# Layer 2's last node stage, moved into its second edge pass

## The chip, the cores and the metric

The kernel runs on one NeuronCore of a Trainium2 chip, in one launch. The metric is the device time of that launch in microseconds (us). The engines of the core run their own instruction streams and wait for one another through semaphores: TensorE (PE, matmuls into the eight PSUM banks; PEld is its weight loads), VectorE (DVE), ScalarE (ACT), GpSimd (POOL) and SyncE (SP, which here only issues DMAs). TensorE's clock is granted by the chip at one of two levels, 1.2 and 2.4 GHz; the profile shows it as 0.50 and 1.00.

## The reference

Four graph layers on one graph of 3125 nodes with 128 features and 50000 edges, sorted by destination. Each layer normalizes its input, applies ReLU, runs a graph operator and adds the result to x. Layer 0 sums weighted neighbours, layer 1 means of neighbours, layer 3 is a diffusion of nine steps over the adjacency, and layer 2 is the one that changes here: two sublayers, each with an eight-headed attention part and a relational part. The second sublayer, cut to what matters:

```python
for h in range(8):                                   # attention part, mean over the heads
    Wh = x1 @ W[h]
    e = leaky_relu((Wh @ a_src[h])[src] + (Wh @ a_dst[h])[dst], 0.2)
    outs.append(segment_sum(seg_softmax(e, dst)[:, None] * Wh[src], dst))
x1 = mean(outs)
deg = segment_sum(w, dst)                            # relational part
x2 = relu(segment_sum((w / maximum(deg[dst], 1e-16))[:, None] * (x2 @ Wc)[src], dst))
x = x + maximum(x1, x2)
h = maximum(layernorm(x), 0)                         # what layer 3 (the diffusion) starts from
```

## The kernel before

Nodes lie in 25 blocks of 128 (the last has 53), edges in 392 chunks of 128. SBUF is one large array, `arena`, addressed by words; `banks` is PSUM.

**An edge pass** is `layer2_edges(i, begin)` (L1439), run once with i = 0 and once with i = 1. GpSimd gathers a chunk's source rows by an indirect DMA (L229, called from L1502) into a ring of 40 chunks, and waits for the sums of chunk c-40 (L1501). SyncE loads the destination terms and indices of a batch of eight chunks (L1515, L1519), three and two batches deep. Batches pass through a chain: one-hot windows and flags (VectorE, L1533 to L1552), logits (L1568), their transpose (PE L1697, ACT L1782), maxima by two scans (L1578, L1584), the exchange at the batch edges (PE L1707 to L1712), `exp` (ACT L1786), transpose back (PE L1719), `spread` of the attention values over the window of 17 nodes (DVE L1618). Then TensorE sums a chunk: in the second pass L1736 (eight heads, 136 columns), L1737 (relational part, 17 columns) and L1739 (softmax sums and degrees, 17 columns); in the first pass L1733 and L1734 (17 columns each) and L1739. ScalarE copies the finished windows into the accumulators `ACC` (nine planes, one for each head and one for the relational part, features by nodes) and `SACC` (L1820, L1823), seven chunks later. All engines walk the same hand-written order of slots, ten to a batch, so that sums of a batch stand some three batches behind its gathers, and each engine works strictly in order.

In the second pass TensorE also runs matmuls whose results nobody reads: `busy` (L1671 to L1675) multiplies an identity into bank 7, with 24 x 512 columns at the start, 3 x 512 a slot until the first sums, and after each chunk's sums 512 + 256 columns:

```python
                            sums(c)
                            busy(512, 256)
```

**The node stage** `layer2_end(begin, ends)` (L2292) starts when all sums of the pass are stored. TensorE first turns `SACC` for all 25 blocks (L1864, 50 instructions), VectorE makes reciprocals (L1869, L1871, L2419). Then block by block: nine products of 128 x 128 x 128 (eight heads with `Wg`, one with `Wc`: L2349, L2352, L2353, L2355, two instructions each), six scalings and a ReLU on ScalarE (L2371, L2374, L2376), two more heads and the sum tree on VectorE (L2426, L2430, L2433, L2435), the maximum (L2438), the residual on GpSimd (L2406), and the layer norm over groups of four blocks (DVE L2444 to L2456, ACT L2381, L2387). `spans` are these groups. SyncE stores the new x by groups (L2326) and brings the adjacency counts back from DRAM over the dead accumulators in five pieces (L2321, L2323, L2330, L2332, L2336, and L2574 in the next stage); `PIECES`, `SOURCES` and `RETURNED` (L2277 to L2280) say which source blocks come with which piece and in which order the diffusion's first step uses them.

**The diffusion** (`diffusion`, L2485) multiplies the adjacency counts (25 source blocks, four ranges of destinations) by the scaled features in nine steps: PE L2640, L2644, L2646. Its first step takes rows that GpSimd, ScalarE and VectorE prepare from the norm's result (L2601, L2699, L2771). `weights_t` (L2218) spreads the softmax of t over TB (PE L2233, DVE L2250) ahead of the second pass; of TB only its last row is read on this path (L2601).

`any_stages` (L3242) is another path, for graphs whose edges are spread too widely; it does not run here.

## Time and profile before

| | |
|---|---|
| median of 3 runs | 2660.73 us (2654.13 to 2671.45) |
| the profiled execution | 2652.48 us, span 2650.7 us, mean granted clock 0.783 |
| busy: PE, PEld | 2346.3 us (89%), 1958.4 us (74%) |
| busy: DVE, ACT, POOL | 1452.3 us (55%), 1208.4 us (46%), 1198.2 us (45%) |
| gathers (L229), second pass | x392, 392.2 us busy |
| PEclk in 40 slices of 66.3 us, tenths of 2.4 GHz | 9856566588755555555698697888899999999999 |

The second edge pass lies at about 1324 to 1873 us of the span, the node stage behind it until 1961, the diffusion until the end. Busy is the time in which an engine had an instruction under way; TensorE's matmuls are pipelined and their ends modelled, so a TensorE that is busy all the time need not stream columns all the time. In a row of a timeline or chain, the first number is the start, the second the duration, x the number of merged instructions, and what stands in brackets the idle time before and who ended it. A group's row gives the busy sum and the mean in ns.

### The profile page before, as it was taken

The numbers are of one execution on the slowest core, as the hardware profiler recorded it, in microseconds if no ns is written. First come the engines' busy times: TensorE is split into PE (matmuls) and PEld (weight loads), VectorE is DVE, ScalarE is ACT, GpSimd is POOL, SyncE is SP. The second block draws the span as 40 slices with busy tenths as digits, with TensorE's granted clock in tenths as the row PEclk, the third lists the DMA queues.
The fourth block names the chain that finished last, engine by engine and source line by source line (L and its number), as shares of the span: only waits on it lengthen the run. The fifth ranks groups of instructions, "written<-read, shape, count | busy, mean of one in ns | idle before, by whom it ended". The sixth has DMA issues, their size and how long they took to land.

```text
span 2650.7 us, 51792 instructions
## 1 busy us (share of the span) xinstructions
PE 2346.3 (89%) x12833; PEld 1958.4 (74%) x12833; DVE 1452.3 (55%) x6161; ACT 1208.4 (46%) x5256; POOL 1198.2 (45%) x1268
## 2 busy tenths in 40 slices
PE   3778778787549999999899999999979999999998
PEld 2555556554339999999857777777878899888887
DVE  5656556578536666666436566665564333344443
ACT  3666667675313333333314343343674444444443
POOL 3777777700067777775077777775131000000000
PEclk9856566588755555555698697888899999999999
DMA  3242442431244444443244344443272000000002
GB/s 90 61 125 64 123 125 64 125 103 42 66 111 113 110 109 108 109 110 106 53 110 110 100 111 108 109 108 85 68 283 83 14 22 18 25 25 25 25 25 61
DMA packets 172291, 227.45 MB, mean 86 GB/s; under 512 B 63503, under 2 KB 131160, under 8 KB 171736
## 3 DMA queue, kind: packets, MB, share of 16 engines
q0 software_dynamic: 50176, 131.74, 18.8%
q1 hardware_dynamic: 114350, 88.60, 11.1%
q10 hardware_dynamic: 7466, 3.73, 0.5%
q8 instruction: 114, 1.87, 0.3%
q14 instruction: 185, 1.52, 0.2%
HBM read 183.63 MB, written 40.29 MB: 84 GB/s over the span
## 4 chain that ended last, share of the span: by engine, by line
PE 71%; issue 7%; DVE 7%; POOL 5%; ACT 4%; DMA 4%; ACTq 2%; DVEq 0%; SPq 0%; POOLq 0%
PE banks L2644 10%; PE banks L2640 10%; PE banks L1675 7%; PE banks L1733 7%; PE banks L1734 6%; POOL arena L229 5%; PE banks L1736 4%; PE banks L1739 3%; PE banks L2646 3%; PE banks L733 2%; PE banks L945 2%; PE banks L1737 2%; DMA arena<-h_table,arena 2%; PE banks L736 2%; PE banks L1691 1%
## 5 line engine op out<-in xcount | busy, mean ns | idle before, releaser
L229 POOL DMA_INDIRECT arena<-value_table,arena x392 | 387.2, 988 | 318.2 <-DMA ed_table<-arena 199.1
L2640 PE MATMUL banks<-counts,u_parts 128*128 128x448 f32 x1323 | 491.7, 372 | 9.6 <-DVE u_parts L2771 9.6
L2644 PE MATMUL banks<-counts_even,u_parts 128*128 128x448 f32 x1323 | 486.3, 368 | 0.0
L229 POOL DMA_INDIRECT arena<-gat_table,arena x392 | 392.2, 1001 | 207.3 <-issue 88.0
L229 POOL DMA_INDIRECT arena<-h_table,arena x392 | 376.3, 960 | 119.4 <-issue 88.4
L2819 DVE CAST counts_even<-counts 128x448 fp32r<-128x448 bf16 x450 | 163.9, 393 | 304.1 <-PE banks L2644 276.1
L733 PE MATMUL banks<-arena 128*128 128x425 bf16 x392 | 198.3, 506 | 84.6 <-ACT arena L789 77.5
L2640 PEld LDWEIGHTS banks<-counts,u_parts 128*128 128x128 f32 x1323 | 249.6, 189 | 30.3 <-issue 9.7
L736 PEld LDWEIGHTS banks<-arena 128*128 128x128 f32 x784 | 211.1, 293 | 80.9 <-issue 72.7
L2644 PEld LDWEIGHTS banks<-counts_even,u_parts 128*128 128x128 f32 x1323 | 249.5, 189 | 20.7 <-ACT counts_even L2747 0.2
L1675 PE MATMUL banks<-arena 128*128 128x256 bf16 (+1 forms) x967 | 262.8, 370 | 1.7 <-DVE arena L2250 1.7
L1734 PE MATMUL banks<-arena 128*128 128x17 f32 x784 | 230.8, 376 | 0.0
L1733 PE MATMUL banks<-arena 128*128 128x17 f32 x784 | 227.2, 371 | 0.0
L786 ACT ACTIVATE arena<-banks 128x400 f32 x392 | 207.9, 530 | 37.2 <-DVE banks L722 26.5
L1820 ACT ACTIVATE arena<-banks 128x32 f32 (+1 forms) x784 | 186.0, 237 | 62.5 <-issue 39.2
L1734 PEld LDWEIGHTS banks<-arena 128*128 128x128 f32 x784 | 214.3, 334 | 0.0
L2747 ACT ACTIVATE counts_even<-counts 128x896 fp32r<-128x896 bf16 x123 | 117.4, 954 | 209.3 <-PE banks L2644 196.6
L1808 ACT ACTIVATE arena<-banks 128x2 f32<-128x2 f32 (+1 forms) x262 | 45.6, 174 | 357.5 <-PE banks L1739 304.3
L1733 PEld LDWEIGHTS banks<-arena 128*128 128x128 f32 x784 | 202.2, 319 | 6.2
L736 PE MATMUL banks<-arena 128*128 128x17 f32 x784 | 174.9, 304 | 35.1 <-DMA arena<-h_table,arena 34.2
L1736 PE MATMUL banks<-arena 128*128 128x136 f32 x784 | 187.5, 325 | 0.0
L722 DVE TENSOR_TENSOR banks<-banks,arena 128x26 f32<-128x26 f32 x391 | 75.7, 194 | 184.4 <-ACT arena L778 180.0
(301 smaller groups left out, 4758.5 us busy)
## 6 DMA issues: line engine op xcount, KB each, us to landing
adj_rows<-arena SPq DMA_DIRECT2D x5, 4000.0 KB
counts<-adj_rows SPq DMA_DIRECT2D x2, 7200.0 KB, 21.6
arena<-ed_table SPq DMA_DIRECT2D x784, 0.5 KB
arena<-turned_rows SPq DMA_DIRECT2D x27, 448.0 KB, 3.4
arena<-h_table,arena POOLq DMA_INDIRECT x392
arena<-value_table,arena POOLq DMA_INDIRECT x392
arena<-gat_table,arena POOLq DMA_INDIRECT x392
counts<-adj_rows SPq DMA_DIRECT2D x2, 1600.0 KB, 6.2
```

Of the source, the lines that this page charges most:

```text
L229: return e.indirect_dma_start(into, None, table, bass.IndirectOffsetOnAxis(ap=index.bitcast(U32), axis=0))
L733: e.matmul(banks[:, c % RBANK, W1:CS], BY_LO[:, kx, :], BY_HI_D[:, kx, 0:CC], start=True, stop=True, skip_group_check=True)
L736: e.matmul(banks[:, c % RBANK, 0:W1], G[:, k, :], S[:, c // BC % 2, c % BC, :], start=False, stop=True, skip_group_check=True).then_inc(l0 ...
L786: e.activation(first.of(C, j), windows_in(j)[:, 1:, 0:WIN], ACT.Copy, scale=SMALL).then_inc(l0_counted, 1)
L1675: e.matmul(banks[:, 7, 0:n], identb, spare[:, 0:n], start=True, stop=True, skip_group_check=True)
L1733: e.matmul(pv[:, 0, :], rows[:, 0:D], OHF[k3][:, j, :], start=begins, stop=True, skip_group_check=True)
L1734: e.matmul(pv[:, 1, :], rows[:, D + H:], OHV[k3][:, j, :], start=False, stop=True, skip_group_check=True)
L1736: e.matmul(pv[:, 0:H, :], rows[:, 0:D], S[c % RS][:, 0:H, :], start=begins, stop=True, skip_group_check=True)
L1820: e.activation(first.of(acc, c), sums_in(c)[:, :, 0:WIN], ACT.Copy).then_inc(e2_acc, 1)
L2640: e.matmul(banks[:, 2 * r, 0:HALFW], weight, C_odd[:, w0:w0 + HALFW], start=start, stop=stop)
L2644: x = e.matmul(banks[:, 2 * r + 1, 0:HALFW], weight, tile(n), start=start, stop=stop)
L2819: e.tensor_copy(into, counts).then_inc(d_even_dve, 1)
```

## The change

- `EndNodes` takes the place of `Ends` and holds the node stage as small steps per block: `products` (three groups of matmuls: heads 0 to 2 with the block's own turn of `SACC`, heads 3 to 6, head 7 and the relational part), `weigh`, `scaled` (three groups of ScalarE scalings that write over the block's own columns of `ACC`), `summed` (the sum tree over `ACC`, maximum, residual, statistics, all on VectorE), and per span `variances`, `root`, `scales`, `normed`.
- `layer2_edges(1, ...)` calls these steps for blocks 0 to 22 within its slots. `first[b]` is the chunk at which block b's steps begin: the chunk after which all its sums are stored, plus eight. Blocks 23 and 24 stay behind the pass, in `layer2_end`. All early blocks use bank 7, one group at a time; the two late ones have banks of their own.
- `busy(512, 256)` after a chunk's sums is called only for chunks below `first[0]`, which is 30. From there on no unread products run.
- x is loaded and stored by spans on SyncE's queue within the pass. The end weights are loaded at the start of the pass, and divided by H there (before: the reciprocals were). GpSimd has no part in the stage any more.
- The counts come back in other pieces: blocks 0 to 12 even when five spans are normed; 18 to 23 when the sums are done; 1 to 17 odd after the last residual; 24 after the last store; 14 and 16 in the diffusion. The order of the sources follows.
- `weights_t` makes only the last row of TB on this path.

```diff
             def sp(e):
                 begin(e)
                 first = Windows(e, FI, f"e2w_{i}")
+                if i:
+                    nodes.begin_sp(e)
                 for b in range(NBATCH):
+                    if i:
+                        for g in nodes.sp_at(b):
+                            nodes.x_store(e, g)
+                            nodes.x_load(e, g + 1)
...
             def dve(e):
...
+                if i:
+                    nodes.begin_dve(e)
                 for p in range(NBATCH + 4):
+                    if i and p == 1:
+                        nodes.degrees(e)
                     for q in range(SLOTS):
                         c = chunk_at.get(SLOTS * p + q)
                         if c is not None:
                             spread(c)
                             if c % PER == 1 and c > 3 * PER:
                                 share(c // PER - 2)
+                            if i:
+                                for b, c0 in nodes.first.items():
+                                    if c == c0 + 2:
+                                        nodes.weigh(e, b)
+                                    if c == c0 + 8:
+                                        nodes.summed(e, b)
+                                        if b % 4 == 3 and b < 20:
+                                            nodes.variances(e, b // 4)
+                                    if c == c0 + 12 and b % 4 == 3 and b < 20:
+                                        nodes.scales(e, b // 4)
...
             def pe(e):
...
                             sums(c)
-                            busy(512, 256)
+                            if not i or c not in nodes.waiting:
+                                if not i or c < nodes.first[0]:
+                                    busy(512, 256)
+                            else:
+                                for b, k in nodes.pe_at(c):
+                                    nodes.products(e, b, k)
...
             def act(e):
...
+                            if i:
+                                for b, k in nodes.act_at(c):
+                                    nodes.scaled(e, b, k)
+                                for b, c0 in nodes.first.items():
+                                    if b % 4 == 3 and b < 20 and c == c0 + 10:
+                                        nodes.root(e, b // 4)
+                                    if b % 4 == 3 and b < 20 and c == c0 + 13:
+                                        nodes.normed(e, b // 4)
...
-        PIECES = [(23, 24), tuple(range(0, 18, 2)), tuple(range(1, 18, 2)) + (22,), (18, 19), (20, 21)]
-
-        SOURCES = PIECES[1] + PIECES[2] + PIECES[0] + PIECES[3] + PIECES[4]
+        PIECES = [tuple(range(0, 14, 2)), tuple(range(18, 24)), tuple(range(1, 18, 2)), (24,), (14, 16)]
+        SOURCES = PIECES[0] + PIECES[1][:3] + PIECES[2] + PIECES[1][3:] + PIECES[3] + PIECES[4]
...
+        class EndNodes:
...
+                self.first = {b: block_end(b) + 8 for b in range(self.EARLY)}
+                self.waiting = {c + k for c in self.first.values() for k in range(7)}
 
...
+            def products(self, e, b, part):
+                weight_sums, eight, last = self.places(b)
+                if part == 0:
+                    if b == 0:
+                        e.wait_ge(d_scales, 2)
+                    elif b < self.EARLY:
+                        self.bank_free(e, b - 1)
+                    e.wait_ge(e2_sacc, NC + block_end(b))
+                    e.matmul(weight_sums, SACC[0:3 * (H + 1), b * P:(b + 1) * P], add_parts[0:3 * (H + 1), :], start=True, stop=True, skip_group_check=True)
+                elif b < self.EARLY:
+                    e.wait_ge(self.copied.sem, self.copied.at(3 * b + part))
+                if part < 2:
+                    for h in ((0, 1, 2), (3, 4, 5, 6))[part]:
+                        x = e.matmul(eight[h], self.own(h, b), end_Wg[:, h, :], start=True, stop=True, skip_group_check=True)
+                else:
+                    e.matmul(last[0], self.own(H - 1, b), end_Wg[:, H - 1, :], start=True, stop=True, skip_group_check=True)
+                    x = e.matmul(last[1], self.own(H, b), end_Wc, start=True, stop=True, skip_group_check=True)
+                x.then_inc(self.product.sem, 1)
+
+            def bank_free(self, e, b):
+                e.wait_ge(self.copied.sem, self.copied.at(3 * b + 3))
+
+            def scaled(self, e, b, part):
+                weight_sums, eight, last = self.places(b)
+                SV = self.SV[b % 2]
+                e.wait_ge(self.product.sem, self.product.at(3 * b + part + 1))
+                if part == 0:
+                    e.wait_ge(self.weighed.sem, self.weighed.at(b + 1))
+                if part < 2:
+                    for h in ((0, 1, 2), (3, 4, 5, 6))[part]:
+                        x = e.activation(self.own(h, b), eight[h], ACT.Copy, scale=SV[:, h:h + 1])
+                else:
+                    e.activation(self.own(H - 1, b), last[0], ACT.Copy, scale=SV[:, H - 1:H])
+                    x = e.activation(self.own(H, b), last[1], ACT.Relu, scale=SV[:, H:H + 1])
+                x.then_inc(self.copied.sem, 1)
+
+            def weigh(self, e, b):
+                do, settle = dve_own.do, lambda: dve_own.settle(e)
+                SV = self.SV[b % 2]
+                e.wait_ge(self.product.sem, self.product.at(3 * b + 1))
+                do(e.tensor_scalar_max(SV, self.places(b)[0], 1e-16))
+                settle()
+                e.reciprocal(SV, SV).then_inc(self.weighed.sem, 1)
+
+            def summed(self, e, b):
+                do, settle = dve_own.do, lambda: dve_own.settle(e)
+                g = self.span_of(b)
+                x = self.XB[:, b - self.SPANS[g][0], :]
+                heads = lambda h, n: ACC[:, h:h + n, b * P:(b + 1) * P]
+                e.wait_ge(self.copied.sem, self.copied.at(3 * b + 3))
+                for n in (4, 2, 1):
+                    do(e.tensor_tensor(heads(0, n), heads(0, n), heads(n, n), ALU.add))
+                    settle()
+                do(e.tensor_tensor(self.own(0, b), self.own(0, b), self.own(H, b), ALU.max))
+                e.wait_ge(self.x_in.sem, self.x_in.at(16 * (g + 1)))
+                settle()
+                e.tensor_tensor(x, x, self.own(0, b), ALU.add).then_inc(self.added.sem, 1)
+                e.wait_ge(self.added.sem, self.added.at(b + 1))
+                do(e.bn_stats(self.stats[b % 2], x))
+                settle()
+                do(e.bn_aggr(self.mv[:, b, :], self.stats[b % 2]))
+
...
+            def begin_dve(self, e):
+                e.tensor_scalar_add(dinv2l, indeg, 1.0).then_inc(self.var.sem, 1)
+                e.wait_ge(self.weights.sem, self.weights.at(32))
+                e.tensor_scalar_mul(end_Wg, end_Wg, 1.0 / H).then_inc(d_scales, 1)
+
...
+            def sp_at(self, batch):
+
+                return [g for g in range(self.NS - 1) if (self.first[4 * g + 3] + 13) // BC + 6 == batch]
+
+            def pe_at(self, c):
+                return [(b, k) for b, c0 in self.first.items() for k in range(3) if c == c0 + 3 * k - k // 2]
+
+            def act_at(self, c):
+                return [(b, k) for b, c0 in self.first.items() for k in range(3) if c == c0 + 2 * k + 2]
+
+        def layer2_end(ends):
...
+            LATE = (NB - 2, NB - 1)
+            G_LATE = ends.NS - 1
...
+                e.wait_ge(ends.made.sem, ends.made.at(G_LATE))
+                returned(0, 0, 7, 0)
+                e.wait_ge(e2_mm, 2 * NC)
+                e.dma_start(counts[:, words(18, 24)], adj_rows[:, words(18, 24)]).then_inc(ends.back[1].sem, 16)
+                e.wait_ge(ends.added.sem, ends.added.at(NB))
+                returned(2, 0, 9, 1)
+                ends.x_store(e, G_LATE)
...
```

## Rows read from the trace of the kernel before

**Rows 1.** Stages: window, length, each engine's busy us (instructions), clock, DMA share, GB/s.

```profile
120.00:540.00 420.00, 323.57 (x1454) 235.61 (x1452) 253.56 (x1322) 278.34 (x1137) 315.37 (x330) 0.60 0.35 102
780.00:1240.00 460.00, 460.00 (x2327) 431.94 (x2327) 283.80 (x1466) 168.50 (x1240) 351.59 (x356) 0.50 0.43 113
1360.00:1438.00 78.00, 78.00 (x580) 58.88 (x578) 46.88 (x232) 29.02 (x187) 59.90 (x60) 1.00 0.42 109
1446.00:1498.00 52.00, 52.00 (x241) 39.77 (x242) 22.93 (x115) 14.25 (x93) 36.71 (x38) 0.50 0.39 101
...
1360.00:1873.00 513.00, 500.82 (x3417) 387.69 (x3414) 305.85 (x1536) 200.87 (x1314) 365.05 (x364) 0.87 0.39 101
...
1873.00:1961.00 88.00, 67.24 (x501) 64.44 (x501) 64.16 (x230) 64.04 (x223) 16.21 (x29) 0.88 0.53 182
1961.00:2650.00 689.00, 670.95 (x3387) 609.46 (x3387) 268.62 (x753) 300.69 (x588) 23.62 (x47) 0.99 0.13 41
```

**Rows 2.** Chain of waits, 1360 to 1873, its shares by line.

```profile
by line: PE banks L1675 35.7%; PE banks L1736 22.1%; PE banks L1737 10.3%; PE banks L1739 8.0%; DMA arena<-gat_table,arena 3.4%; issue 3.4%; POOL arena L229 2.8%; PE banks L1697 2.1%; PE banks L1707 1.9%; PE banks L1691 1.7%; PE banks L1719
```

**Rows 3.** The gathers of the second pass, their source line.

```profile
L229 POOL DMA_INDIRECT arena<-gat_table,arena x392: 940/946/2021, 1324.4 to 1839.6; - x196
  issue: 88.0, 289
  PE banks L1739: 35.8, 102
```

**Rows 4.** Line L1739 in the window 1100 to 2100.

```profile
L1739 PE MATMUL banks<-arena x534: 181/183/197, 1100.8 to 1872.3; 128*27 128x17 bf16 x178
```

**Rows 5.** Chain of waits, 1873 to 1962.

```profile
1875.63 10.83 PE banks L1864 x50
...
1890.98 1.14 ACT arena L2371 x4
...
1958.51 1.25 ACT arena L2387 x3
...
1960.77 0.70 PE banks L2640
```

**Rows 6.** Timeline of TensorE in the node stage.

```profile
1886.39 2.07 PE L2349 MATMUL banks<-arena 128*128 128x128 f32 x8
1888.26 1.06 PE L2352 MATMUL banks<-arena 128*128 128x128 f32 x4
...
1889.88 1.06 PE L2349 MATMUL banks<-arena 128*128 128x128 f32 x8
```

**Rows 7.** Groups by line, 1873 to 1961.

```profile
L2426 DVE TENSOR_TENSOR arena<-arena 128x384 f32<-128x384 f32 x25 | 13.8, 551 | 2.0 <-ACT arena L2374 2.0
...
L2438 DVE TENSOR_TENSOR arena<-arena 128x128 f32<-128x128 f32 x25 | 7.3, 292 | 2.6
...
L2362 ACT ACT_TABLE_LOAD x1 | 1.3, 1283 | 0.0
```

**Rows 8.** DMA issues, 1870 to 2100: KB each, us to landing.

```profile
counts<-adj_rows SPq DMA_DIRECT2D x2, 7200.0 KB, 21.6
```

**Rows 9.** Timeline of TensorE ahead of the clock's fall.

```profile
1440.75 0.30 PE L1697 MATMUL banks<-arena 128*64 128x128 f32 x1 [1.18 <-DVE arena L1570]
```

**Rows 10.** Windows of line L1739 alone, one instruction per chunk.

```profile
780.00:1240.00 460.00, 68.58 (x351) 35.15 (x351) 0.50 0.43 113
1360.00:1406.00 46.00, 5.65 (x31) 2.83 (x31) 1.00 0.41 109
```

**Rows 11.** Timeline of TensorE in the first pass.

```profile
1000.79 0.61 PE L1733 MATMUL banks<-arena 128*128 128x17 f32 x2
1001.24 0.59 PE L1734 MATMUL banks<-arena 128*128 128x17 f32 x2
```

**Rows 12.** Timeline of TensorE in the second pass, low clock.

```profile
1463.01 0.82 PE L1736 MATMUL banks<-arena 128*128 128x136 f32 x2
1463.63 0.45 PE L1737 MATMUL banks<-arena 128*128 128x17 f32 x2
```

More of the change, by code:

```diff
@@ L2216, in build, with weights_t @@
         U_parts = rounded("u_parts", U_at, UW)
-        def weights_t(begin, bank, room):
+        def weights_t(begin, bank, room, rows=tuple(range(STEPS))):
             def sp(e):
@@ new lines, in home, with own, places @@
+            def home(self, b):
+                if b < 12:
+                    return self.own(H - 1, b)
+                return self.spare if b == 12 else self.own(H, b - 13)
+            def own(self, h, b):
+                return ACC[:, h, b * P:(b + 1) * P]
+            def places(self, b):
+                n = {NB - 2: (7, 0, 2), NB - 1: (3, 4, 5)}.get(b, (7, 7, 7))
+                first = [banks[:, n[0], (q + 1) * D:(q + 2) * D] for q in range(3)]
+                second = [banks[:, n[1], q * D:(q + 1) * D] for q in range(4)]
+                return banks[:, n[0], 0:H + 1], first + second, [banks[:, n[2], q * D:(q + 1) * D] for q in range(2)]
```

294 lines of the change are left out of this document (121 added, 173 removed).

## The prediction

> **What bounds the kernel now.** I read the stages first, then the chain of waits inside the stage that changes, then single instructions. The stage table [rows 1] shows two edge passes of the same loop and the node stage behind the second one. The first pass (780 to 1240 shown) has TensorE busy for all 460 us at a granted clock of 0.50, that is 1.2 GHz. The second (1360 to 1873) takes 513 us, with TensorE busy 501, VectorE 306 and ScalarE 201. Then comes the node stage from 1873 to 1961, then 689 us of diffusion. The chain through the second pass [rows 2] is TensorE nearly everywhere, and its largest item is L1675, the products that nobody reads (35.7%). Behind TensorE stands a second limit that is nearly as near: the gathers [rows 3]. One takes 0.946 us and is followed by 0.30 us (88.0 us in 289 cases), so 1.25 us a chunk. The 392 gathers start between 1324.4 and 1839.6, against 391 x 1.25 = 489 us at their own pace: they lose only 26 us to TensorE.
>
> So taking work from TensorE in the pass can win little there. The change has two separate effects: the 88 us behind the pass shrink, and TensorE inside the pass gets other work and perhaps another clock.
>
> **Removed behind the pass.** The last L1739 of the pass starts at 1872.3 [rows 4], the first diffusion product at 1960.77 [rows 5]: 88.5 us. What stays: the last stores to the accumulators until 1875.6, where L1864 begins [rows 5] (3.3 us); two blocks of products; one block's scaling, sums and norm. A block's products are 9 matmuls, each two instructions. At the low clock eight of them run from 1886.39 to 1888.26 [rows 6], 1.87 us, so 18 take 4.2, plus two of the 50 of L1864 (10.83/50 each), 0.43: 4.7 us. From 1889.88 the same eight take 1.06 in place of 2.07: such a run brought the clock back within 3.5 us, so the second block costs about half: 7.2 for both. ScalarE's last two scalings are 0.6 (four take 1.14, [rows 5]). The sums of a block on VectorE: a 384-wide add is 0.551, a 128-wide one 0.292 [rows 7], hence 0.68 + 0.42 + 3 x 0.29 for the tree, the maximum and the residual, and 0.45 for statistics and aggregation (my estimate, from the 128-wide row): 2.4, with the waits between them 2.6. Then the root with its table load (1.28, [rows 7]; Exp is used in the pass, so it is loaded anew) 1.5, inverse and shift 0.7, five norms 2.1 (three take 1.25, [rows 5]) and 1.1 to the first diffusion product. Sum 3.3 + 7.2 + 0.6 + 2.6 + 1.5 + 0.7 + 2.1 + 1.1 = 19 us. **Gain: 69 us**, whatever happens in the pass.
>
> The diffusion's input moves too. Its returned pieces are now seven blocks issued before the pass ends, six when the sums are done, nine after the last residual. A piece of nine takes 21.6 us [rows 8]; diffusion consumes a source block in 689/(9 x 25) = 3.06 us and reaches the nine as its eleventh source, 31 us after its start, while they are issued 5 us before it. That is covered by 14 us: 0; without that cover the rest of the 21.6 would show.
>
> **Added inside the pass, with no clock change.** Per block (16 chunks) TensorE gets 18 + 2 instructions, ScalarE nine scalings (2.6 us), a share of root and norm and of two table loads (some 1.2), VectorE 2.6 plus 0.5 for the weights. ScalarE at 201 of 513 us and VectorE at 306 of 513 carry that. The SP queue gets two weight loads, six x loads and five stores; the stores wait for a norm that is due one or two batches before the queue's loads are needed (three buffers), so nothing: if that cover went, it would be a landing of some 2 us per group of blocks, 10 us in all. begin on VectorE waits for the end weights (issued first), hidden by the first batch of gathers. The t-weights shrink from ten products to one; nobody on the path waits: 0. The POOL queue loses the 25 residual adds, off the path here.
>
> **The clock in the pass is the disputed term.** Removed from chunk 30 on: 512 + 256 columns a chunk. What do the traces show of TensorE without them? The first pass is the same loop without such products, and 0.50 all the way, with TensorE 100% busy [rows 1]. The first stage (120 to 540) has a 425-column product per chunk and 0.60. The second pass with them has 1.00 from 1360 to 1438, and 0.50 from 1446 to 1498 [rows 1], busy in both: after one gap of 1.18 us before L1697 [rows 9] the clock went down, and it was still down at 1498, 52 us on, though each chunk carried its sums and its 768 extra columns. So even with the extra products the clock is barely held. Without them a chunk's sums stream less than half as much, and the new products come in runs of three, four and two heads, 0.9 to 1.9 us at the low clock, with whole chunks between. The run that brought the clock back behind the pass [rows 6] was up to 3.5 us of nothing else. I take 0.50 for nearly all of the pass from chunk 30 on.
>
> The Trainium skill's page "TensorE: Matmul & The Clock Gate", in the table of "Why this matters for your kernels", asks only that there be no long idle gap, longer than any that this pass would have, between bursts of matmuls. By it the clock would stay up here, which is the first rival. The trace does not agree: the clock fell behind a gap of 1.18 us [rows 9], and was low through a pass without one.
>
> **TensorE's pace at 0.50.** The first pass did 351 chunks in 460 us [rows 10]: 1.311 a chunk, 20.97 for 16. The second pass has the same weight loads and wider moving sides. Where no unread product stands before it, L1736 takes 0.62 until L1737 starts, against 0.45 from L1733 to L1734; L1737's two last 0.45, L1734's 0.59 [rows 11, 12]: +0.17 - 0.14 = +0.03 a chunk, so 21.5. With a block's products (4.7): 26.2 us for 16 chunks, where the gathers need 20.0. TensorE is then the bound by a wide margin.
> One more wait: VectorE runs a block's sums in one piece at chunk c0+8, after ScalarE's last scaling, and queued behind it are flags, one-hot and scans, and the next spreads, for which TensorE waits. TensorE has about three chunks of work ready then (3.4 us); VectorE needs the scaling (1.2), 2.6, and a handful of its own operations. I put 1.5 us a block, between 0 (hidden, as VectorE was until now) and 2.6 (the whole piece exposed), nearer the upper end because those operations come on top.
>
> 27.7 x (362/16 = 22.6) = 627 us from chunk 30, which is at 1405.8 (the 31st L1739 starts just before 1406, [rows 10]); less 3 us for the first stretch at the high clock: the sums end at 2030 instead of 1873. **Loss: 157 us.**
>
> **Sum.** 157 - 69 = +88 us on the profiled execution's 2652.5 (span 2650.7 and 1.8 around it): 2740. That execution is 8 us under the median of the three runs shown (2660.7) and inside their spread; I leave it at **2740 us**, 3% slower. With the stall at 0: -34; at 2.6: +25. So this case spans 2705 to 2770.
>
> **Rival 1, the clock holds (faster).** If the products of the finished blocks and the sums together keep 1.00, TensorE needs under 15 us for 16 chunks (0.91 a chunk now at that clock, less the unread ones, plus 2.5) and the gathers set the pace: the last one starts between 1814 and 1840 and the sums end 25 us later (33 now, less 0.25 for each of the last 30 chunks). Diffusion begins 17 to 19 us on, between 1857 and 1883, 78 to 104 us earlier: 2549 to 2575, say 2562. For it: the 0.60 of the first stage, where node products also lie between the chunks, and the 0.88 of the node stage. Against it: the first pass and the fall at 1442 [rows 1, 9]. The skill's page named above speaks for it. It decides from where about half of the 16-chunk stretches run at the gathers' 20.0: (1960.8 - 19 - 1405.8)/22.6 = 23.7 us a stretch is break-even between 27.7 and 20.0. Chance 0.18.
>
> **Rival 2, a mixed clock.** The runs of products lift it now and then, as in the first stage. With a third of the stretches at 20.0: 25.1 on average, 567 us, sums end at 1973, diffusion at 1992: 31 later: 2684 (2650 to 2705). For it: the 0.60 of the first stage. Against it: that stage streams 425 columns a chunk at one pass and 512-wide products, the new one has no such width. Chance 0.12.
>
> **Rival 3, the waits are worse than priced.** weigh, scaled and the three product groups each wait on another engine through one bank (7), so that a wait of 1 us at each of the three would add 23 x 3 = 69 us to the low-clock case: over 2775. Nothing in the trace speaks for it; enough chunks lie between the steps. Chance 0.04.
>
> The forecast has the rest, 0.66.
>
> **How the numbers follow.** A measurement of this kernel can tell about 1%, 27 us. Faster by more than that (under 2634): rival 1, 0.18. Within (2634 to 2687): about half of rival 2 and a little of the forecast's lower edge, 0.08. Slower: 0.74. The range must leave out rival 1 whole; it reaches from rival 2's lower end to a little beyond the forecast's upper bound, 2650 to 2780. The forecast's own range is 2705 to 2770.
>
> **What would show it.** Granted clock in the pass: 0.50 for nearly all of it (rival 1: near 1.0). Gathers: the last one starts near 2000, and their idle time before a launch is given to L1739, several hundred us in place of 35.8. From the last L1739 to the first L2640: 19 us. TensorE's waits on VectorE before the spreads: 1.5 us a block. The prediction fails if the clock holds for more than half of the pass, or if the pace at the low clock without the unread products is not that of the first pass.

## The result, and the profile after

| | us, median | ratio to before, 95% |
|---|---|---|
| before | 2657.43 (2649.32 to 2671.45) | 1 |
| after | 2739.27 (2737.97 to 2742.29) | 1.0304 (1.0258 to 1.0350) |
| forecast | 2740 (2650 to 2780) | |

The change makes the kernel 3% slower. The ratios, here and below, leave out executions in the slower state that the chip sometimes shows (one of run 10's ten, at 2685.11 us), and need not be the quotients of the medians. The profiled execution of after has a span of 2737.1 us, 86.4 more than the 2650.7 of before. Line numbers have moved: L1736, L1737 and L1739 of before (a chunk's sums) are L1762, L1763 and L1765 now.

The stages of after, in the columns of [rows 1]:

```profile
780.00:1240.00 460.00, 459.61 (x2319) 431.05 (x2319) 281.90 (x1463) 168.13 (x1235) 351.83 (x356) 0.50 0.43 113
1360.00:1406.00 46.00, 45.05 (x312) 32.67 (x316) 23.60 (x117) 13.07 (x84) 35.04 (x37) 0.99 0.43 112
1406.00:1600.00 194.00, 181.12 (x897) 169.92 (x895) 111.25 (x525) 80.83 (x458) 115.31 (x118) 0.52 0.34 89
1600.00:1800.00 200.00, 182.63 (x915) 171.82 (x915) 113.83 (x538) 86.75 (x475) 114.12 (x117) 0.53 0.34 88
1800.00:2000.00 200.00, 183.46 (x916) 172.68 (x915) 112.41 (x526) 87.21 (x476) 95.07 (x96) 0.53 0.36 103
2047.00:2737.00 690.00, 671.34 (x3387) 609.23 (x3387) 268.48 (x754) 301.15 (x588) 24.08 (x47) 0.99 0.13 42
```

Up to chunk 30 the clock is as in [rows 1]; the chunk itself comes at 1408.4, 2.6 us later than the 1405.8 of before. From there the granted clock is 0.52 to 0.53 where the whole pass before had 0.87. It is 0.50 from 1412.5 on, but for four short rises of 6.8 us each; two of them, and a stretch between:

```profile
1610.50:1617.00 6.50, 3.78 (x31) 3.39 (x29) 4.47 (x18) 2.87 (x17) 4.60 (x5) 1.00 0.30 78
1617.50:1692.00 74.50, 70.53 (x347) 66.48 (x346) 42.35 (x203) 32.84 (x179) 42.53 (x43) 0.50 0.35 90
1692.50:1699.00 6.50, 3.93 (x32) 3.54 (x31) 4.54 (x19) 2.85 (x17) 4.64 (x5) 1.00 0.32 83
```

The diffusion is as it was: 690 us at 0.99. The pass ends later, and what follows it is short. The last of the sums:

```profile
L1765 PE MATMUL banks<-arena x784: 182/195/196, 770.4 to 2028.0; 128*27 128x17 bf16 x196
```

The timeline of TensorE behind it, up to the first diffusion product (L2732):

```profile
2030.77 0.56 PE L2392 MATMUL banks<-arena 27*128 27x9 f32 x2 [2.62 <-ACT arena L1856]
2031.27 3.35 PE L2397 MATMUL banks<-arena 128*128 128x128 f32 x14
...
2035.93 2.39 PE L2397 MATMUL banks<-arena 128*128 128x128 f32 x14
...
2047.15 0.71 PE L2732 MATMUL banks<-counts,u_parts 128*128 128x448 f32 x1 [8.39 <-DVE u_parts L2862]
```

The sums end 155.7 us later than in [rows 4] (1872.3), and 19.2 us lie behind them in place of 88.5: +155.7 - 69.3 = +86.4, the whole difference of the spans.

The gathers, which answer to [rows 3], with what ended GpSimd's idle time before them in this pass, and TensorE's waits between 1406 and 2028 (engine, line, what it waited for: us in all, times, longest):

```profile
L229 POOL DMA_INDIRECT arena<-gat_table,arena x392: 940/946/1806, 1325.2 to 1963.2; - x196
  PE banks L1765: 194.4, 212
```

```profile
PE banks L1762 <- DVE arena L1630: 30.5, 23, 2.8
PE banks L1765 <- DVE arena L1643: 14.4, 43, 1.1
PE banks L1745 <- ACT arena L1819: 2.9, 3, 1.5
```

A gather is as fast as before (946 ns at the median), but the last one starts 124 us later: they now follow TensorE, for which they wait 194.4 us in place of 35.8. TensorE waits once per finished block for spread weights from VectorE (L1630), and a little for the split weights (L1643). Most of the waits for L1630 are of 1.05 to 1.27 us; four, each at the end of one of the short rises of the clock, are of 2.40 to 2.77.

### The profile page after: what moved, and what is told of

The parts are those of the page before. It is cut to its first block, busy times and chain, and to the rows that moved or that the text cites. A ratio compares the mean times of both kernels' runs of the same rounds, so it can differ in the third digit from the quotient of the medians.

```text
span 2737.1 us, 50328 instructions
## 1 busy us (share of the span) xinstructions
PE 2392.2 (87%) x12048; PEld 2082.9 (76%) x12091; DVE 1462.8 (53%) x6184; ACT 1236.2 (45%) x5318; POOL 1176.5 (43%) x1243
## 4 chain that ended last, share of the span: by engine, by line
PE 70%; DVE 9%; issue 8%; ACT 4%; POOL 4%; DMA 3%; ACTq 1%; DVEq 0%; SPq 0%; POOLq 0%
PE banks L2736 9%; PE banks L2732 9%; PE banks L1759 6%; PE banks L1760 6%; PE banks L1762 6%; POOL arena L229 4%; PE banks L1765 3%; PE banks L2397 3%; PE banks L2738 3%; PE banks L733 2%; PE banks L945 2%; PE banks L1763 2%; DMA arena<-h_table,arena 2%; PE banks L1717 2%; PE banks L736 2%
## 5 line engine op out<-in xcount | busy, mean ns | idle before, releaser
L229 POOL DMA_INDIRECT arena<-gat_table,arena x392 | 386.1, 985 | 336.5 <-PE banks L1765 194.4
L2732 PE MATMUL banks<-counts,u_parts 128*128 128x448 f32 x1323 | 491.2, 371 | 8.4 <-DVE u_parts L2862 8.4
L1762 PE MATMUL banks<-arena 128*128 128x136 f32 x784 | 283.7, 463 | 30.5 <-DVE arena L1630 30.5
L2732 PEld LDWEIGHTS banks<-counts,u_parts 128*128 128x128 f32 x1323 | 249.2, 188 | 29.5 <-issue 8.6
L736 PEld LDWEIGHTS banks<-arena 128*128 128x128 f32 x784 | 211.7, 293 | 71.3 <-issue 61.7
L1762 PEld LDWEIGHTS banks<-arena 128*128 128x128 f32 x784 | 194.3, 304 | 39.8 <-DVE arena L1630 32.6
L1760 PEld LDWEIGHTS banks<-arena 128*128 128x128 f32 x784 | 214.2, 333 | 0.0
L1759 PEld LDWEIGHTS banks<-arena 128*128 128x128 f32 x784 | 202.1, 319 | 6.5
L1763 PEld LDWEIGHTS banks<-arena 128*128 128x128 f32 x784 | 207.0, 316 | 0.0
## 6 DMA issues: line engine op xcount, KB each, us to landing
counts<-adj_rows SPq DMA_DIRECT2D x1, 7200.0 KB, 21.4
```

The costliest lines, as they stand in the source:

```text
L229: return e.indirect_dma_start(into, None, table, bass.IndirectOffsetOnAxis(ap=index.bitcast(U32), axis=0))
L736: e.matmul(banks[:, c % RBANK, 0:W1], G[:, k, :], S[:, c // BC % 2, c % BC, :], start=False, stop=True, skip_group_check=True).then_inc(l0 ...
L1759: e.matmul(pv[:, 0, :], rows[:, 0:D], OHF[k3][:, j, :], start=begins, stop=True, skip_group_check=True)
L1760: e.matmul(pv[:, 1, :], rows[:, D + H:], OHV[k3][:, j, :], start=False, stop=True, skip_group_check=True)
L1762: e.matmul(pv[:, 0:H, :], rows[:, 0:D], S[c % RS][:, 0:H, :], start=begins, stop=True, skip_group_check=True)
L1763: e.matmul(pv[:, H, :], rows[:, D + H:], S[c % RS][:, H, :], start=False, stop=True, skip_group_check=True)
```

## The experiments

All ratios are to the kernel before, run on the same chip. "The pass" is the second edge pass; runs 7 and 8, on a chip apart, stand in their section.

| kernel | us | ratio, 95% | clock in the pass | last sums product |
|---|---|---|---|---|
| 1: unread products kept in 9 of 16 chunks | 2784.28 | 1.0467 (1.0425 to 1.0510) | 0.50 to 0.57 | 2086.4 |
| 2: before, without unread products | 2667.77 | 1.0038 (1.0015 to 1.0060) | 0.50 to 0.52 | 1886.5 |
| 3: VectorE's sum two chunks later | 2732.17 | 1.0277 (1.0239 to 1.0315) | 0.50 to 0.54 | 2029.1 |
| 4: three of nine products | 2687.68 | 1.0124 (1.0087 to 1.0161) | 0.50 to 0.52 | 1973.0 |
| 5: unread in every chunk | 2805.89 | 1.0532 (1.0477 to 1.0586) | 0.62 to 0.71 | 2105.6 |
| 6: unread in every chunk, wider | 2809.31 | 1.0553 (1.0516 to 1.0589) | 0.69 to 0.71 | 2113.0 |
| 9: the change again | 2738.57 | 1.0298 (1.0253 to 1.0344) | 0.53 | 2027.2 |
| 11: sum in four pieces, no unread | 2707.97 | 1.0174 (1.0130 to 1.0218) | 0.50 to 0.54 | 1998.6 |
| 10: unread and four pieces | 2664.60 | 0.9996 (0.9960 to 1.0032) | 0.85 to 1.00 | 1946.3 |
| 12: unread and pieces off the split | 2603.43 | 0.9785 (0.9761 to 0.9809) | 0.98 to 1.00 | 1887.4 |

### 1. Unread products back in the chunks without node work

```
-    if not i or c < nodes.first[0]:
-        busy(512, 256)
+    if i:
+        for b, c0 in nodes.first.items():
+            if c == c0 + 7:
+                nodes.bank_free(e, b)
+    busy(512, 256)
```

> The changed kernel, with 512 + 256 unread columns again after every chunk's sums outside the seven chunks of a block's products (so in 9 of 16 chunks), TensorE waiting for the block's last scaling before the first of them. Theory (the low clock makes the loss): the granted clock in the pass comes back to 0.8 to 0.9, the sums end near 1880 instead of 2028, the tail of 19 us stays, so about 2590 us (2565 to 2625), faster than the kernel before. Rival A (the stage's clock is low whatever is added, unread products only take time): 201 chunks times 0.45 to 0.64 us more, 2830 to 2870. Rival B (waits between the engines set the pace, the clock does not matter): about 2739, no change.

Measured: 2784.28 us, 45 more than after. The windows (columns as above):

```profile
1406.00:1600.00 194.00, 185.88 (x940) 156.78 (x939) 101.63 (x480) 73.88 (x420) 106.94 (x108) 0.57 0.31 82
1600.00:1800.00 200.00, 196.59 (x933) 164.67 (x933) 104.11 (x488) 79.47 (x431) 104.13 (x104) 0.52 0.30 79
```

The clock stayed low, so my theory of this run was wrong: to undo the removal in nine chunks of sixteen does not undo its effect. The unread products were paid for, at the low clock, but not in full: the pass is 58.4 us longer than that of after (2086.4 against 2028.0), where rival A had 90 to 129, and the time lies between rivals A and B. In the same pass TensorE's waits for L1630 fell from 30.5 to 10.1 us, which is a part of the difference.

### 2. The kernel before, without unread products from chunk 30

```
-    busy(512, 256)
+    if not i or c < 30:
+        busy(512, 256)
```

> The kernel before, with its unread products left out from chunk 30 on and nothing else changed. Theory: the clock falls to 0.50 right behind chunk 30 and TensorE sets the pace with 21.5 us for 16 chunks: 362/16 x 21.5 = 486 us, sums end at 1892 instead of 1873, so +19: about 2675 us (2660 to 2685), a small loss. Rival A (unread products only cost time): the gathers set the pace, sums end between 1840 and 1850, 2625 to 2635. What lies between this and the changed kernel is then the price of the node work at the low clock.

Measured: 2667.77 us, 0.4% slower than before.

```profile
1406.00:1600.00 194.00, 194.00 (x985) 181.66 (x984) 121.24 (x601) 78.26 (x510) 148.31 (x151) 0.52 0.42 110
1600.00:1800.00 200.00, 200.00 (x994) 188.16 (x993) 121.97 (x607) 78.81 (x511) 148.02 (x153) 0.50 0.41 108
1415.00:1886.00 471.00, 471.00 (x2325) 442.72 (x2325) 279.91 (x1389) 184.62 (x1201) 316.69 (x324) 0.50 0.37 98
```

```profile
L1739 PE MATMUL banks<-arena x784: 182/195/196, 772.3 to 1886.5; 128*27 128x17 bf16 x196
```

This is the removal alone, and two things are to be seen. The clock is 0.50 from 1415 to the end of the sums, with TensorE busy in all 471 us: it fell without a wait and did not come back. And the price is only 14.2 us of pass, 4.0 of them ahead of chunk 30 (1409.8 here, 1405.8 in before). The reason is in the pace: at 0.50 the sums alone take 21.4 us for 16 chunks, in each of the twenty stretches of 16 from chunk 46 to 366, about as long as the gathers of before (515.2 us for 391, [rows 3], or 21.1 for 16). So the removal costs little by itself, but it leaves no room for the node products.

### 3. VectorE's sum of a block two chunks later

```
-    if c == c0 + 8:
+    if c == min(c0 + 10, NC - 1):
         nodes.summed(e, b)
```

Root, scales and norms move by two chunks too.

> The changed kernel, with VectorE's sums of a block two chunks later (c0+10, at most chunk 391), the root, inverse and norm two later too. Theory: VectorE no longer waits for ScalarE's last scaling (65 us in the pass in 23 waits), so most of TensorE's 30.5 us of waits for the spreads in the pass goes: 20 to 30 us less, 2710 to 2720. Rival (the spreads are late because of the length of the sums themselves, not of their wait): 0 to 8 us less.

Measured: 2732.17 us, 7 less than after; the rival was right. The wait moved:

```profile
PE banks L1765 <- DVE arena L1643: 36.9, 43, 2.9
```

The waits for L1630 are gone and those for the split weights are 22.5 us longer. The sum is one piece of VectorE's work; wherever it stands whole, something that TensorE needs is queued behind it.

### 4. Three of nine products per block

```
-    for h in ((0, 1, 2), (3, 4, 5, 6))[part]:
+    for h in (((2,), (6,))[part] if b < self.EARLY else ((0, 1, 2), (3, 4, 5, 6))[part]):
```

and the product of head 7 only for the last two blocks. The output is not the layer's.

> The changed kernel, with only three of the nine products of each of the blocks 0 to 22 made (one in each of the three groups; six matmuls a block are left out, and the numbers are not the layer's). Theory (TensorE at the low clock sets the pace): 23 x 12 instructions x 0.234 us = 65 us less, about 2675. Rival B (waits between the engines set the pace): under 15 us less. Rival C (the products lift the clock here and there): the clock of 0.53 in the pass falls to 0.50 and the gain is under 50.

Measured: 2687.68 us, 51.6 less than after, at a clock of 0.50 to 0.52. The pass ends 55.0 us earlier (1973.0), where the theory had 65 for the products left out: TensorE's time for them is on the path, for the most part. Rival C's sign came too: the four short rises of the clock in after are missing here. They were worth little (see the stall, below), and the gain in the pass is above the 50 that this rival had as its bound.

### 5 and 6. Unread products in every chunk

Bank 7 isn't free while node products stand in it, so these multiply by zeros and add to the current bank of sums:

```
+    if i and c >= nodes.first[0]:
+        for n in (384, 384):
+            e.matmul(banks[:, bank_of(c), 0:n], spare[:, 0:P], spare[:, 0:n], start=False, stop=True)
     e.wait_ge(e2_split, nb0 + b + 1)
```

The second kernel has (512, 512) in the seven chunks of a block's node work.

> The changed kernel, with two products of 384 columns (768 columns, as many as in the kernel before) inside the sums of every chunk from the first finished block on, the seven chunks with a block's node work among them. They multiply by zeros and add to the bank of sums that TensorE owns at that moment, ahead of the wait for the split weights, so nothing is changed in the output and no other engine's bank is touched. The run with such products in only 9 of 16 chunks stayed at a granted clock of 0.50 to 0.57 and cost 45 us more than the change. Theory (it is the stretches of seven chunks with fp32 products and nothing wide streamed that lose the clock, so filling them too keeps it): clock 0.80 or more in 1406 to 1800, the gathers are paced by themselves again, the last sums product near 1875 to 1890 (kernel before 1872.3), the work behind the pass 19 us as after the change, so 2590 to 2610 us, faster than the kernel before by about 50 to 65. Rival A (the fp32 products of the node work hold the clock down whatever stands beside them): clock 0.50 to 0.55, every chunk 0.64 us dearer, the pass some 80 us longer than in the changed kernel: 2810 to 2860. Rival B (the clock is up in some stretches and down in others): 0.6 to 0.8, 2640 to 2740.

> As the run with two products of 384 columns in every chunk, but two of 512 columns (1,024) in the seven chunks of a block's node work. If the width beside the fp32 products matters, the clock is higher than in that run (by 0.05 or more in 1406 to 1800), and if the clock is already near 0.99 there, the time is the same within 5 us. If both stay at 0.50 (rival A), it is 15 to 35 us slower than that run, by 7 chunks of 16 times 256 more columns at 1.2 GHz (0.21 us) times 22.6 blocks = 34 us.

Measured: 2805.89 and 2809.31 us. The clock is not low any more, it goes up and down (rival B of the first, at another time than it gave):

```profile
1600.00:1800.00 200.00, 187.89 (x1057) 132.76 (x1055) 106.92 (x506) 79.32 (x436) 105.96 (x108) 0.71 0.31 82
```

The cause of the falls is in the timeline of TensorE, here around 1666:

```profile
1663.43 0.29 PE L1763 MATMUL banks<-arena 128*128 128x17 f32 x2
1663.57 0.49 PE L1766 MATMUL banks<-arena 128*128 128x384 bf16 x2
1663.99 0.18 PE L1768 MATMUL banks<-arena 128*27 128x17 bf16 x1
...
1664.99 0.18 PE L1768 MATMUL banks<-arena 128*27 128x17 bf16 x1
1666.58 0.72 PE L1762 MATMUL banks<-arena 128*128 128x136 f32 x2 [1.40 <-DVE arena L1630]
...
1674.78 0.20 PE L1768 MATMUL banks<-arena 128*27 128x17 bf16 x1
...
1676.54 0.20 PE L1768 MATMUL banks<-arena 128*27 128x17 bf16 x1
```

Before the wait a chunk with its two unread products (L1766) takes 1.00 us, behind it 1.76: windows of 1655 to 1665 and of 1668 to 1680 have a clock of 1.00 and 0.50. VectorE's own timeline says why TensorE waited:

```profile
1662.81 1.48 DVE L2437 TENSOR_TENSOR arena<-arena 128x512 f32<-128x512 f32 x3 [2.04 <-ACT arena L2419]
...
1665.37 0.18 DVE L2446 BATCH_NORM_AGGREGATE arena<-arena 128x2 f32<-128x6 f32 x1
1665.48 0.28 DVE L1560 TENSOR_TENSOR arena<-arena 64x129 f32<-64x129 f32 x1
...
1666.22 0.30 DVE L1630 TENSOR_TENSOR arena<-arena 128x153 f32<-128x153 bf16 x1
```

It waited 2.04 us for ScalarE's last scaled product, then ran the sum in one piece until 1665.55, then four operations of a batch's scan, and only then the spread weights. Between 1406 and 2100 the clock fell 17 times from 1.00 to 0.50, each time at such a wait of 1.40 to 1.62 us (the expectation of run 7 has 18, a miscount). It rose again 20 to 55 us later. Three shorter waits for L1630 at the high clock, of 0.75 to 0.98 us, did not lose it. So two things of the change bear on the clock: with unread products in every chunk it comes back, to stay until the next such wait, with them in 9 of 16 or none it doesn't, but for rises of mostly 7 us; and in run 5 each of these long waits loses it. The wider kernel does nothing more: its mean clock from 1406 to 1800 is 0.70 against 0.68, and its time is 3.4 us longer, no difference.

### 7 and 8. VectorE's sum in four pieces, with and without unread products

The tree's first add, its other two, maximum and residual, and the statistics stand behind the 9th, 10th, 11th and 12th chunk of the block; root, scales and norms follow later.

```
-    if c == c0 + 8:
-        nodes.summed(e, b)
+    for k in range(4):
+        if c == min(c0 + 9 + k, NC - 1):
+            nodes.summed(e, b, k)
```

> As the run with two products of 384 columns in every chunk, and VectorE's sum of a block (2.0 us of waiting for ScalarE's last scaled product and 2.7 us of instructions in one piece behind one chunk) in four pieces, behind the 9th to the 12th chunk of the block, with what hangs on it later. In the run without this, each of the 18 falls of the clock from 1.00 to 0.50 between 1406 and 2086 stands at a wait of TensorE for VectorE's spread weights (L1630) of 1.40 to 1.62 us, one per block, and at 0.50 a chunk with its unread products takes 1.77 us, at 1.00 only 1.0, against 1.28 of a gather's pace. Theory (the stall behind VectorE's sum is what loses the clock, the unread products are what keeps it): the waits are under 1 us, the clock 0.85 or more in 1406 to 2000, the gathers set the pace, last sums product 1875 to 1895, 2590 to 2615 us. Rival A (with that wait gone another of the same length comes in its place, for VectorE's split weights as in the run with the sums two chunks later): clock 0.6 to 0.75, 2760 to 2810. Rival B (the clock falls without such a wait, from the fp32 products): clock under 0.6, 2820 or more.

> The changed kernel (no unread products) with VectorE's sum of a block in the same four pieces. At a clock of 0.50 the waits for VectorE in the pass are 30.5 + 14.4 us of TensorE's time; where the pieces take most of that away, 15 to 30 us less than the changed kernel: 2710 to 2725. The theory says that the clock stays at 0.50 to 0.55 here, as nothing wide is streamed. Rival (without the stalls the clock holds even without unread products): 0.8 or more, 2590 to 2640.

Measured: 2998.01 us (ratio 0.9955, 0.9931 to 0.9978) and 2969.52 (0.9863, 0.9824 to 0.9903), on a chip on which the kernel before takes 3015.11. There all passes are longer, the first one too (its gathers run from 39.7 to 637.3 us, in after from 40.8 to 533.6), though a single gather lasts as long (946 ns at the median). Times of that chip can't be set beside the others, so both kernels were run again, with the change itself.

### 9 to 11. The change, and both kernels again

> The changed kernel itself once more, to stand beside the two other kernels of this call. The last call ran on a chip on which the kernel before takes 3015 us instead of 2655 to 2661, with a third edge pass that is longer than here, so its ratios can't be set against those of the others. Expected where the kernel before takes about 2660: a ratio of 1.026 to 1.035, 2730 to 2750 us. If the chip is the slow one again: near the 0.986 of the kernel with VectorE's sum in four pieces, above it by 0 to 0.01.

> Two products of 384 columns in every chunk and VectorE's sum of a block in four pieces, as in the last call; there the clock was 0.79 in 1600 to 1990 instead of 0.57 without the unread products, and 0.62 to 0.72 with them but with the sum in one piece. Where the kernel before takes 2660: theory (VectorE's stall loses the clock): clock 0.75 to 0.95 in 1500 to 2000, last sums product 1880 to 1960, 2600 to 2680 us. Rival (another wait of over 1 us per block takes its place): clock 0.6 to 0.72, 2760 to 2810 as with the sum in one piece (2805.9).

> The changed kernel with VectorE's sum of a block in four pieces and no unread products, as in the last call, where the clock stayed 0.50 in nearly all of the pass. Where the kernel before takes 2660: 2710 to 2725 us (the 30.5 + 14.4 us of waits for VectorE in the pass mostly gone), clock 0.50 to 0.55. Rival: the waits move as in the run with the sums two chunks later, 2730 to 2740.

Measured: 2738.57, 2664.60 and 2707.97 us. First the pieces without unread products:

```profile
1600.00:1800.00 200.00, 197.68 (x965) 186.91 (x964) 121.82 (x575) 90.72 (x502) 123.54 (x124) 0.50 0.35 92
```

```profile
PE banks L1766 <- DVE arena L1643: 8.5, 23, 1.1
```

30.6 us less than the change, as its theory had it, a little better than the range it gave: the waits for VectorE fell from 30.5 + 14.4 to 8.5 us. The clock is 0.50 although TensorE is busy for 198 of 200 us and its only wait of 0.6 us or more from 1400 to 1980 is one of 1.13 at 1413.44, where the clock fell. Now the same with unread products:

```profile
1406.00:1500.00 94.00, 89.55 (x688) 64.64 (x687) 66.74 (x318) 49.30 (x282) 71.76 (x73) 1.00 0.43 112
1600.00:1800.00 200.00, 192.35 (x1274) 137.37 (x1273) 127.57 (x604) 94.38 (x527) 129.86 (x131) 0.85 0.37 98
```

The clock is up for most of the pass, and the ratio is 0.9996 against 1.0532 with the same unread products and the sum in one piece. That VectorE's sum in one piece cost the clock is shown by this pair (run 5 and run 10): they differ in nothing but where the sum and what hangs on it stand. Eight falls of the clock are left between 1500 and 1910. Four follow a wait for the split weights of 0.94 to 1.20 us, one (1509.92) a wait of 0.98 with no releaser in the profile. The other three follow waits for the split weights of only 0.52 to 0.58, while thirteen more waits for them of 0.51 to 0.62 in the pass had no fall behind them. One of each kind:

```profile
1602.03 0.18 PE L1769 MATMUL banks<-arena 128*27 128x17 bf16 x1 [0.94 <-DVE arena L1643]
...
1628.98 0.18 PE L1769 MATMUL banks<-arena 128*27 128x17 bf16 x1 [0.52 <-DVE arena L1643]
```

The windows around the second:

```profile
1626.00:1631.00 5.00, 4.49 (x37) 3.05 (x38) 4.63 (x20) 1.65 (x12) 4.02 (x4) 1.00 0.42 106
1632.00:1651.00 19.00, 19.00 (x86) 13.97 (x85) 7.25 (x37) 5.08 (x30) 7.96 (x9) 0.50 0.28 73
```

### 12. Pieces kept away from the split weights

```
-    if c == min(c0 + 9 + k, NC - 1):
+    if c == nodes.piece_at(b, k):
...
+    def piece_at(self, b, k):
+        light = [c for c in range(self.first[b] + 10, NC) if c % BC in (2, 3, 4, 5, 6)] + [NC - 1] * 4
+        return light[k]
```

> Two products of 384 columns in every chunk, and the four pieces of a block's VectorE sum placed only behind the third to seventh chunk of a batch of eight, from the block's 10th chunk on, so that none stands in front of the split weights that TensorE needs for a batch's first chunk. In the run with the pieces behind the 9th to 12th chunk five of the falls of the clock between 1500 and 1910 stand at a wait of TensorE for the split weights of 0.94 to 1.20 us, or (1509.92) at one of 0.98 that the profile puts down to no releaser; the last sums product was at 1946.3 there, at 1872.3 in the kernel before. Theory (those waits lose the clock): they fall under 0.6 us, the clock is 0.90 or more in 1500 to 1900, last sums product 1890 to 1925, 2600 to 2640 us, faster than the kernel before. Rival (with the wait gone the products of the node work lower the clock by themselves, or another wait does): clock 0.80 to 0.88, last sums product 1935 to 1960, 2645 to 2670, no different from the kernel before.

Measured: 2603.43 us (2597.75 to 2606.83), ratio 0.9785 (0.9761 to 0.9809). This version is faster than both kernels: by 2.1% (1.9 to 2.4) than before and, by the two ratios (0.9785 / 1.0298), by 5% than the change. The next three views are its windows, its last sums product, and its first diffusion product in the timeline of TensorE.

```profile
1406.00:1500.00 94.00, 91.38 (x694) 66.77 (x695) 68.13 (x328) 49.23 (x280) 72.36 (x72) 0.98 0.42 109
1500.00:1600.00 100.00, 96.25 (x739) 69.59 (x739) 71.74 (x344) 55.16 (x309) 75.81 (x77) 1.00 0.45 118
1600.00:1800.00 200.00, 192.30 (x1482) 139.45 (x1481) 146.22 (x701) 108.16 (x610) 150.51 (x150) 1.00 0.43 112
```

```profile
L1769 PE MATMUL banks<-arena x784: 182/189/197, 768.5 to 1887.4; 128*27 128x17 bf16 x196
```

```profile
1905.51 0.71 PE L2744 MATMUL banks<-counts,u_parts 128*128 128x448 f32 x1 [8.90 <-DVE u_parts L2874]
```

The pass is 15.1 us longer than before (1887.4 against 1872.3, [rows 4]) and what follows takes 18.1 us in place of 88.5, 70.4 less; together -55.3, and the spans differ by 2595.9 - 2650.7 = -54.8. With the clock held, TensorE does the node products beside the gathers, and the gain behind the pass is kept.

What held it is less clear than the time. The theory had the waits for the split weights under 0.6 us, and they aren't: five of 0.70 to 0.90 are left, and four of 1.10 to 1.21 for ScalarE (L1822) have come, which run 10 hasn't. In all TensorE waits 17.0 us in this pass (12.0 for L1643, 5.0 for L1822), against 19.6 in run 10. Behind only one of these waits did the clock fall, and for 3.4 us:

```profile
1493.34 0.18 PE L1769 MATMUL banks<-arena 128*27 128x17 bf16 x1 [0.84 <-DVE arena L1643]
...
1751.23 0.18 PE L1769 MATMUL banks<-arena 128*27 128x17 bf16 x1 [0.90 <-DVE arena L1643]
```

```profile
1494.00:1499.00 5.00, 5.00 (x28) 4.12 (x27) 2.90 (x14) 2.21 (x9) 3.81 (x4) 0.66 0.43 111
```

That the placement of the pieces keeps the clock is shown by runs 10 and 12; that it does so by shorter waits is not.

## Why the prediction was right, point by point

**The work behind the pass.** Forecast 19 us, measured 19.2; the gain of 69 is 69.3. The diffusion's late pieces cost nothing: 690 us against 689 [rows 1].

**The clock.** Forecast 0.50 for nearly all of the pass from chunk 30, measured 0.52 to 0.53. My grounds were two, and both hold. The first pass was the pattern: without unread products the sums don't keep the clock; run 2 shows that for this pass, with no node work in it. And the node products don't bring it back: 0.50 in run 11, nearly without a wait. For the second I leaned on [rows 6], as if 3.5 us of products alone had brought the clock back; the 10.83 us of L1864 stand right before them [rows 5], with no gap between. I hadn't seen that the change also brings a second cause, the wait behind VectorE's sum (runs 5 and 10); in the change itself it ended each of the four short rises.

The Trainium skill's page "TensorE: Matmul & The Clock Gate" (table of "Why this matters for your kernels") asks for no long idle gap between bursts. The trace doesn't agree: run 11 has no gap over 1.13 us from 1400 to 1980 and is at 0.50 from 1500 on, and run 2 is at 0.50 with TensorE busy for 471 us of 471. The measurement decides.

**The pace at 0.50 without node work.** Forecast 21.5 us for 16 chunks. Run 2 has 21.4 in all its stretches but the first (18.5, partly at the high clock) and the last (20.1).

**The products.** Forecast 4.7 us a block. Six of the nine, with two instructions each, were 2.8 of it and gave 55.0 / 22.6 = 2.4 in run 4. Run 11, with few waits, has 26.2 at the median for a stretch of 16 chunks (26.1 to 26.4 but for the first and last); less 0.4 of waits (8.5 / 22.6) and run 2's 21.4 that leaves 4.4.

**The stall.** Forecast 1.5 us a block, from VectorE's sum in one piece. The one wait is 1.33 in the mean (30.5 / 23), which is what I priced, and 1.07 in most blocks; the waits for the split weights and for L1819 (14.4 and 2.9) I didn't see, and all three are 47.8 / 22.6 = 2.1 a block. The terms as measured, 21.4 + 4.4 + 2.1 = 27.9, are 0.3 to 0.4 more than the 27.55 that a stretch of after has at the median. The trace has a place for most of it: the four waits at the end of the short rises are together 10.3 us, 6.0 more than four of 1.07, or 0.3 a block, and they cost nothing, since from one such wait to the next three of these blocks take 26.7 to 26.9 us and the fourth 27.7, no more than the others. There TensorE did a block's work sooner and then waited longer for the same VectorE. The sum was right to 2 us (2030 against 2028.0) partly by luck: the pace and the products were put 0.1 and 0.3 a block too high, the stall 0.6 too low, and the pass reached chunk 30 2.6 us later than before.

**A sign that I had wrong.** I expected the last gather near 2000; it starts at 1963.2, 64.8 us ahead of the last sums. A gather waits for the sums of 40 chunks earlier, which at 27.5 us for 16 is 69 us: the sign didn't follow from my own sum. Nothing in the forecast hung on it.

**The rivals.** Rival 1 (clock holds, 2549 to 2575) is not what the change does; run 12, with unread products and another placement, comes near it, at 2603. Its last gather starts at 1837.5, inside the 1814 to 1840 that I had, and its gathers wait 30.2 us for TensorE in this pass, no more than the 35.8 in [rows 3]. But its sums end 49.9 us behind the last gather, at 1887.4, where I had 25 us and 1839 to 1865: I had put TensorE, without unread products, under 15 us for 16 chunks, and in run 12, which makes them, most stretches take 21.0 or 21.1. Rival 2, a mixed clock, is what runs 5 and 6 show, but slower than the change and not faster: unread products cost 0.64 us a chunk (1.76 less the 1.12 from L1765 to L1765 in after at 1705) wherever the clock is down, a term that rival hadn't. Rival 3 (waits through bank 7) didn't come.

## What to carry to other kernels

Work that moves from behind a pass into it has to be priced at the clock that the pass will have after the change, not at the one it has now; here that is 4.4 us a block, or about half of it at the high clock by [rows 6]. Products that nobody reads were 35.7% of the chain [rows 2], and yet removing them alone gained nothing (run 2): look for the same loop without them in the same trace, as [rows 1] has it. And a step that is put into another engine's queue goes in pieces of the size of its neighbours, away from what the bound engine waits for: that alone was worth 31 us at the low clock; with the clock at stake it took the ratio from 1.0532 to 0.9996, and the second placement to 0.9785, though why that one held the clock is open.

## What I had not expected of the hardware

- **A wait and the clock.** In run 12 TensorE waited 1.21 us and the clock stayed at 1.00, in run 10 it waited 0.94, and elsewhere 0.52, and the clock fell. The first, with the windows of 6 us around it:

```profile
1758.76 0.27 PE L1746 MATMUL banks<-arena 64*128 64x64 f32 x1 [1.21 <-ACT arena L1822]
```

```profile
1752.00:1758.00 6.00, 5.55 (x42) 4.13 (x42) 3.89 (x20) 4.10 (x15) 4.25 (x5) 1.00 0.38 96
1758.00:1764.00 6.00, 5.24 (x43) 3.81 (x44) 3.87 (x15) 4.43 (x27) 4.19 (x5) 1.00 0.68 193
1764.00:1770.00 6.00, 6.00 (x45) 3.93 (x44) 5.11 (x27) 2.63 (x17) 4.62 (x5) 1.00 0.43 110
```

  The length of the wait alone doesn't decide. What does was not settled.
- **Chips differ.** On one chip the kernel before took 3015 us instead of 2655 to 2661, and there the four pieces without unread products (2969.52) beat those with them (2998.01), the other way round than on the chip of runs 9 to 11 (2707.97 and 2664.60). Its traces put many waits down to issue or to no releaser of this core; the cause is open.
